# Transpositions of a two-layer FFN and attention kernel moved from TensorE to 16-bit DMA transposes

## The reference

```python
x = x + 0.5 * ffn(layernorm(x))          # 8 experts, hidden 256, all experts computed for all tokens
x = x + attention(layernorm(x))          # 8 heads of width 8, causal
x = x + 0.5 * ffn(layernorm(x))          # the same weights as the first
# ffn: logits = RMS-normalised xf @ gate_w.T + gate_b; g = top-1 of softmax(logits / 0.5)
#      norm_g = g / (g + 1e-6); h = gelu(xf @ w1 + b1); out = sum over experts of (h @ w2 + b2) * norm_g
# attention: layernorm again with weights, qkv = xn @ w_qkv; q, k scaled to unit length;
#      softmax(8 * q k^T, causal) @ v; @ w_out
```

## Time and profile before

| | us |
|---|---|
| median of 3 runs | 272.5 (272.35 to 272.63) |
| the profiled execution, its own time | 272.64 |
| its span in the profile | 271.2 |
| TensorE busy | 262.1 |
| VectorE busy | 220.5 |
| ScalarE busy | 218.8 |
| GpSimd busy | 81.1 |
| first FFN layer, by the windows | 8.7 to about 105 |
| attention | about 106 to 176 |
| second FFN layer | about 177 to 267 |

### The profile page before, as it was taken

One profiled execution on the slowest core, in us unless ns is written; L12 is line 12 of the kernel. 1 busy time (PEld: TensorE's weight loads), 2 busy tenths in 40 slices (PEclk: granted clock), 3 DMA queues, 4 the chain that ended last, 5 costly groups with the idle time before them and its releaser, 6 DMA issues.

```text
span 271.2 us, 5570 instructions
## 1 busy us (share of the span) xinstructions
PE 262.1 (97%) x1893; PEld 187.6 (69%) x1893; DVE 220.5 (81%) x599; ACT 218.8 (81%) x345; POOL 81.1 (30%) x178
## 2 busy tenths in 40 slices
PE   8999999999999999979998999999999999999995
PEld 7876878888788786533434534278888887888783
DVE  7999899998898979795687687478889678698784
ACT  2797678868877879999899999977777868859673
POOL 6202204214850483663148536430200000200100
PEclk9999999999999999999999999999999999999999
DMA  4641200001000100100010002300004211200311
GB/s 147 198 142 24 57 1 2 0 1 39 2 1 0 44 0 0 36 8 0 4 41 2 1 4 70 82 8 1 0 2 116 40 39 41 40 27 12 71 48 39
DMA packets 24895, 9.42 MB, mean 35 GB/s; under 512 B 15682, under 2 KB 24100, under 8 KB 24868
## 3 DMA queue, kind: packets, MB, share of 16 engines
q1 hardware_dynamic: 24724, 9.01, 13.4%
q10 hardware_dynamic: 144, 0.07, 0.1%
HBM read 4.88 MB, written 2.62 MB: 28 GB/s over the span
## 4 chain that ended last, share of the span: by engine, by line
PE 77%; ACT 6%; DVE 6%; issue 5%; POOL 4%; DMA 1%; POOLq 0%; DVEq 0%; ACTq 0%
PE ps L582 10%; PE ps L600 10%; PE ps L588 10%; PE ps L605 10%; PE ps L585 9%; PE ps L603 9%; PE ps L763 7%; ACT probs L968 3%; PE ps L725 3%; PE ps L797 2%; POOL probs L1593 2%; POOL w_raw L1587 2%; PE ps L702 1%; ACT h L955 1%; PE ps L543 1%
## 5 line engine op out<-in xcount | busy, mean ns | idle before, releaser
L955 ACT ACTIVATE h<-ps,cols 128x512 f32<-128x512 f32 x128 | 87.9, 694 | 35.8 <-PE ps L588 32.2
L1133 DVE TENSOR_TENSOR h_lo<-h,h_hi 128x512 fp32r<-128x512 f32 x128 | 88.1, 695 | 19.1 <-ACT h_hi L958 16.7
L968 ACT ACTIVATE probs<-ps 128x1024 f32<-128x1024 f32 (+1 forms) x80 | 65.4, 911 | 2.7 <-PE ps L725 2.5
L582 PE MATMUL ps<-xT_hi,w_hi 128*128 128x512 f32 x128 | 51.5, 402 | 0.0
L600 PE MATMUL ps<-h_hi,w_hi 128*128 128x512 f32 x128 | 50.6, 395 | 0.3 <-ACT yT L980 0.3
L605 PE MATMUL ps<-h_lo,w_hi 128*128 128x512 f32 x128 | 50.2, 392 | 0.0
L958 ACT ACTIVATE h_hi<-ps,cols 128x512 fp32r<-128x512 f32 x73 | 50.2, 688 | 0.0
L588 PE MATMUL ps<-xT_lo,w_hi 128*128 128x512 f32 x128 | 50.0, 390 | 0.0
L585 PE MATMUL ps<-xT_hi,w_lo 128*128 128x512 f32 x128 | 49.8, 389 | 0.0
L603 PE MATMUL ps<-h_hi,w_lo 128*128 128x512 f32 x128 | 49.8, 389 | 0.0
L763 PE MATMUL ps<-probs,v_ones 128*32 128x512 f32 (+4 forms) x384 | 34.2, 458 | 1.2 <-POOL probs L1593 1.0
(11 more groups left out here) (151 smaller groups left out, 288.5 us busy)
## 6 DMA issues: line engine op xcount, KB each, us to landing
w_raw<-in_L_ffn_w SPq DMA_DIRECT2D x8, 256.0 KB, 4.9
turned<-blocks SPq DMA_DIRECT2D x6, 256.0 KB, 2.1
w_raw<-turned SPq DMA_DIRECT2D x24, 64.0 KB, 2.3
w_raw<-v_ones SPq DMA_DIRECT2D x8, 128.0 KB, 2.4
x_sb<-in_L_attn_x SPq DMA_DIRECT2D x3, 256.0 KB, 7.3
out_x<-x_sb SPq DMA_DIRECT2D x3, 256.0 KB, 2.3
w_raw<-o_scaled SPq DMA_DIRECT2D x2, 256.0 KB, 4.5
x_sb<-in_L_attn_x SPq DMA_DIRECT2D x2, 128.0 KB, 2.2
```

The source lines that it names most:

```text
L582: pe.matmul(bank, w1_hi[:, w], xT_hi[:, cols_g], start=True, stop=False)
L955: first = nc.scalar.activation(h[:, slot, :], ps[:, BANK_H + slot, :], ACT.Gelu, bias=bias)
L968: nc.scalar.activation(probs[:, s % P_SLOTS, :, 0:width], ps[:, bank:bank + 2, 0:width], ACT.Exp, scale=SCALE).then_inc(exp_done, 1)
L1133: dve.tensor_tensor(h_lo[:, slot, :], h[:, slot, :], h_hi[:, slot, :].bitcast(f32), ALU.subtract).then_inc(split_done, 1)
```

## The change

1. The stacks of all four groups are turned by a DMA (`dma_start_transpose`, 16-bit, one for q and one for k, issued by SyncE after the group's `stack_done`). TensorE's transpositions, the four jobs, and the copies to `qT` and `kT` go; the layouts of `qT`, `kT`, `sq`, `qk_raw` and the small tensors change so that each operand is contiguous by group. `unit_vectors` becomes one instruction.
2. Three 128x512 tiles of fp32 are turned in another way: y of group 0, the attention norm of group 0, and the features (FFN norm) of group 3. GpSimd copies the tile as 16-bit halves in two planes (`make_planes`), SyncE turns the planes by one DMA, GpSimd joins them (`join_planes`) to `landed` or `xf`.
3. The order changes with it: the residual of group 0 to c = 6 and 7 of group 1, its attention statistics to 8 and 9, its norm to 12 and 13; the affine of its features, its qkv products and its copies into group 2; `high_stacks` of both groups into group 3; the jobs and the stacks of group 2 to earlier or later quads; GpSimd's program is written out.

```diff
-AT_ONE = dict(AT, gate_product=0)
-AT_THIRD = dict(AT, qk_transpose=13, q_copy=13, k_copy=13, ln_normalise=(2, 3), ln_transpose=5, ln_copy=5, ln_low=7,
-                att_normalise=(10, 11), qk_high=9, gate_product=5, gate_logits=6, gate_shift=12, gate_tanh=13, gate_weight=14)
+AT_ONE = dict(AT, gate_product=0, residual=(6, 7), att_stats=(8, 9), att_aggregate=10, att_normalise=(12, 13))
+AT_THIRD = dict(AT, ln_normalise=(2, 3), ln_transpose=5, ln_copy=5, ln_low=7,
+                att_normalise=(10, 11), gate_product=0, gate_logits=1, gate_shift=12,
+                first_affine=2, first_qkv=4, qk_squares=5, qk_copy=6, qk_sums=6, qk_guesses=7, gate_tanh=13, gate_weight=14)
...
-               qk_copy=1, qk_guesses=1, qk_high=8, qk_transpose=12, q_copy=12, first_scores=12)
+               qk_copy=1, qk_guesses=1, first_high=0, qk_high=9, first_scores=12)
...
-        jobs = [(q1, "ln", LAST), (q1 + 1, "project", (0, 0)), (q1 + 4, "project", (0, 1)),
-                (q1 + 5, "qkv", 0), (q1 + 6, "qkv", 1), (q1 + 7, "q_stack", LAST - 1), (q1 + 8, "k_stack", LAST - 1),
-                (q2, "q_stack", LAST), (q2 + 1, "k_stack", LAST), (q2 + 3, "ffn_ln", 0),
+        jobs = [(q1, "ln", LAST), (q1 + 2, "project", (0, 0)), (q1 + 4, "project", (0, 1)),
+                (q1 + 5, "qkv", 0), (q1 + 7, "qkv", 1), (q2 + 3, "ffn_ln", 0),
...
# SyncE
+            for n in range(3):
+                sp.wait_ge(planes_done, n + 1)
+                if n:
+                    sp.wait_ge(joined, n)
+                sp.dma_start_transpose(planes_t[:, :, :].rearrange("p w (t q) -> p (w t) q", q=P),
+                                       planes[:, :, :].rearrange("p w c -> p (w c)")).then_inc(planes_in[n], 16)
...
+                sp.wait_ge(stack_done, 2 * p + 2)
+                for turned_stack, stack in ((qT, q_stack), (kT, k_stack)):
+                    sp.dma_start_transpose(turned_stack[:, p, :, :].rearrange("p a (t q) -> p (a t) q", q=P),
+                                           stack[:, :, :].rearrange("p h r -> p (h r)")).then_inc(stacks_in[p], 16)
...
# ScalarE
+                if F == PLANED_FFN:
+                    act.wait_ge(xf_done[FFN], F + 1)
...
+                if p == PLANED_ATT:
+                    act.wait_ge(joined, 2)
+                    normed = landed[:, :]
...
# GpSimd
+            def make_planes(n, made, count, words):
+
+                pool.wait_ge(made, count)
+                if n:
+                    pool.wait_ge(planes_in[n - 1], 16)
+                pool.tensor_copy(planes[:, :, :], by_plane(words)).then_inc(planes_done, 1)
+
+            def join_planes(n, words):
+                pool.wait_ge(planes_in[n], 16)
+                return pool.tensor_copy(by_plane(words), planes_t[:, :, :])
...
+                if layer == 0 and g == 1:
+                    make_planes(0, y_evac, PLANED_Y + 1, yT[:, :])
+                    ln_once(2)
+                    join_planes(0, landed[:, :]).then_inc(joined, 1)
+                    gate_root(1)
+                    ln_twice(0)
+                    make_planes(1, xn_done[ATT], GROUP_TILES, xn[:, ATT, :, :].rearrange("p t d -> p (t d)"))
+                    ln_once(3)
+                if layer == 0 and g == 2:
+                    pool.wait_ge(resid, GROUP_TILES)
+                    join_planes(1, landed[:, :]).then_inc(joined, 1)
+                    make_planes(2, xn_done[FFN], GROUP_TILES * PLANED_FFN + GROUP_TILES,
+                                xn[:, FFN, :, :].rearrange("p t d -> p (t d)"))
+                    pool.wait_ge(gate_mm, PLANED_FFN)
+                    pool.wait_ge(xT_ready, PLANED_FFN)
+                    join_planes(2, xf[:, FFN, :]).then_inc(xf_done[FFN], 1)
+                    ln_twice(1)
+                    gate_root(2)
+                    inverse_lengths(pool, 0)
+                    unit_vectors(pool, 0)
+                if layer == 0 and last:
+                    low_parts(pool, 0)
+                    inverse_lengths(pool, 1)
+                    ln_twice(2)
+                    unit_vectors(pool, 1)
+                    low_parts(pool, 1)
+                    gate_root(3)
```

More of the change, by code:

```diff
@@ L190, in build @@
         blocks = sb("blocks", [P, GROUP])
+        u16 = mybir.dt.uint16
+        planes = sb("planes", [P, 2, GROUP], u16)
+        planes_t = sb("planes_t", [P, 2, GROUP], u16)
+        landed = sb("landed", [P, GROUP])
         turned_dram = [nc.dram_tensor(f"turned{n}", (P, GROUP), f32, kind="Internal").ap() for n in range(TURNS)]
@@ L232, in build @@
         o_zero = sem("o_zero")
+        planes_done, joined = sem("planes_done"), sem("joined")
+        planes_in = [sem(f"planes_in{n}") for n in range(3)]
         job_filled, job_emptied = sem("job_filled"), sem("job_emptied")
@@ L424, in low_features, with q_and_k, raw_tiles @@
             eng.tensor_tensor(xT_lo[:, part], features(F), xT_hi[:, part].bitcast(f32), ALU.subtract).then_inc(xT_ready, 1)
+        def q_and_k(qkv):
+            return qkv[:, :, 0:2 * INNER].rearrange("p t (w c) -> p t w c", c=ROW)
+        def raw_tiles(buffer, first):
+            return buffer[:, :, first:first + 2, :].rearrange("p w t c -> p t w c")
         def unit_vectors(eng, p):
@@ L635, in ffn_group @@
                         down(layer, F, 0)
-                        if operands and not first:
-                            y_transposes(F - 1, ln_groups=F + 1, att_groups=g - 1)
+                        if operands and g > 1:
+                            y_transposes(F - 1, ln_groups=LAST, att_groups=2 if last else 0)
                     if layer == 1 and first and c == 3:
@@ L913, in square_qk @@
                 for half, qkv in qkv_halves(p):
-                    nc.scalar.activation(sq[:, 2 * half:2 * half + 2, :], qkv[:, :, 0:2 * INNER], ACT.Square).then_inc(sq_done, 1)
+                    nc.scalar.activation(raw_tiles(sq, 2 * half), q_and_k(qkv), ACT.Square).then_inc(sq_done, 1)
             def copy_qkv(p):
@@ L918, in copy_qkv @@
                 for half, qkv in qkv_halves(p):
-                    nc.scalar.activation(qk_raw[:, 2 * half:2 * half + 2, :], qkv[:, :, 0:2 * INNER], ACT.Copy)
+                    nc.scalar.activation(raw_tiles(qk_raw, 2 * half), q_and_k(qkv), ACT.Copy)
                 if p == 0:
@@ L1073, in normalise @@
                 dve.wait_ge(rstd_done[kind], n + 1)
-                if n <= GROUPS:
-                    dve.wait_ge(ln_t[kind], n)
+                if kind == ATT and n:
+                    dve.wait_ge(planes_done, 2)
+                    dve.wait_ge(ln_t[ATT], n - 1)
+                elif kind == FFN and n == GROUPS:
+                    dve.wait_ge(planes_done, 3)
+                elif kind == FFN and n < GROUPS:
+                    dve.wait_ge(ln_t[FFN], n)
                 for i in tiles:
@@ L1166, in residual @@
                     xi = x_tile(g, i)
-                    y = y_rows(F) if landed else ps[:, bank, :]
+                    y = y_rows(F) if by_blocks else landed if F == PLANED_Y else ps[:, bank, :]
                     dve.scalar_tensor_tensor(xi, y[:, P * i:P * i + P], gate_half[:, F % 2, i:i + 1], xi,
@@ L1393, in empty @@
                     t0 = GROUP_TILES * LAST + halves[arg][0]
-                    dve.tensor_copy(qk_raw[:, halves[arg][0]:halves[arg][1] + 1, :], qkv[:, :, 0:2 * INNER])
+                    dve.tensor_copy(raw_tiles(qk_raw, halves[arg][0]), q_and_k(qkv))
                     for quad in range(QUADS):
@@ L1537, in ffn_group @@
                     ln_once(2 * GROUPS - 1)
-                if third:
-                    low_parts(pool, g - 2)
-                if layer == 0 and g == 1:
-                    ln_twice(g - 1)
-                    ln_once(F + 2)
             pool.memset(ones[:, :], 1.0).then_inc(const_self, 1)
```

222 lines of the change are left out of this document (83 added, 139 removed).

## The result

| | before | after |
|---|---|---|
| median (lowest to highest), us | 272.56 (272.35 to 272.63) | 275.96 (275.29 to 275.99) |
| ratio to before | | 1.012, 95% interval 1.0102 to 1.0138 |
| the profiled execution, its own time | 272.64 | 275.93 |
| its span | 271.2 | 274.2 |

The change made the kernel slower by 1.2%, 3.4 us, where the forecast was 0.8 us faster. The time lies near that of rival A (276.3 us), but not for the reason that A gave. The mean granted clock is 0.994.

What follows compares the result with a forecast made beforehand. TensorE (97% busy) was taken to bound the kernel, ScalarE's exponentials 108 to 134 us, both nearly thereafter. Layer -2.4, attention -1.2, stall +2.3, group 3 +0.4 sum to -0.9 us: 271.7 us, range 269.8 to 279 us.

Steps and rivals of the forecast that it cites:

- rival A: Transposing DMA takes 4.5 us, as the copy in short pieces; stall 5.9 us, total 276.3 us; chance 0.30.
- Stall 2.3 us: Group 2: TensorE waits 1.9 us for gelu 9 ahead of chunk 9's down-product, plus 0.4 us for backlog.
- the backlog: Group 2, after the stall: ScalarE still owes the qkv copies and VectorE its sums, 0.4 us more.
- C + T + C: Turns 2 and 3: GpSimd split, transposing DMA, GpSimd join, one after another; each GpSimd copy C taken as 1.2 us.
- T: Time of a 256 KB transposing DMA from issue to landing: taken as 2.5 us, between 2.1 and 11.3 us.
- VectorE's splits are early ... I count 0: Group 1: bunched residual, statistics and norm use some 1.5 us of split slack; counted 0, up to 1 us loss.
- Group 3: Attention's rstd stands ahead of the unit vectors on GpSimd, ScalarE's slot is a chunk later: 0.4 us lost.
- Attention: TensorE's 2.2 us of transpositions count only where ScalarE waits for scores, 134 to 151 us: 1.2 us gained.
- Groups 2 and 3 have over 5 us: Stacks' DMAs of groups 2 and 3 land with over 5 us to spare, so they are hidden.
- B: Rival: the DMA transposes blocks one by one, T near 11 us, stall 19 us, total near 300 us; chance 0.08.
- C: Rival: waits covered, GpSimd copy near 1.0 us, T 2.1 us, stall 0.3 us, total 268.9 us; chance 0.12.
- D: Rival: attention gives nothing, its waits come back elsewhere, the layer's gain is eaten: +0.3, 272.8 us; chance 0.15.

Runs made afterwards that it cites:

- experiment 10: Stacks-only kernel plus six SBUF to SBUF DMAs in SyncE's idle time (transposes of 1, 2, 4, 8 blocks; two plain 256 KB copies): 269.67 us.
- Experiment 3: Changed kernel plus eleven unused 128x128 fp32 products on TensorE between up 12 and down 9 of group 2: 275.19 us.
- Experiment 1: Changed kernel with ScalarE's rounding of group 3's features moved from chunk 5 to 9 of group 2, VectorE's low part from 7 to 11: 272.24 us.
- experiment 8: Stacks-only kernel plus five unneeded GpSimd copies of 128x1024 halves in group 1, where GpSimd's queue is idle: 274.03 us.
- experiment 5: Kernel of Experiment 1 with VectorE's low part of the features at chunk 9 instead of 11: 271.56 us.
- experiment 4: Changed kernel with only the stacks turned by DMA; y, norm and features turned by TensorE at the places of before: 269.69 us.
- experiment 6: Stacks-only kernel plus y of group 0 turned by planes, joined at once, with VectorE's residual at chunks 3 and 4: 270.5 us.
- experiment 9: Kernel of experiment 6 with planes split and joined by ScalarE instead of GpSimd: 270.8 us.

## Why the prediction was wrong

Right was the mechanism: where the stall comes, who makes it (two waits in ScalarE's queue, seen as 2.31 and 4.00 us), and the order in which norm, turn, affine, norm, turn and rounding follow each other. The term that failed is "Stall 2.3 us" (1.9 for the stop and 0.4 for the backlog): both together measured 6.3 us. What the traces have for it, in the prediction's own pieces:

| piece | predicted | measured |
|---|---|---|
| attention norm of group 0 done | 58.7 | 59.7 |
| first C + T + C | 4.9 | 6.0 (59.74 to 65.71) |
| affine, gelu 6 and rounding, split, norm 3 | 3.3 | 3.4 |
| second C + T + C | 4.9 | 5.6 (69.10 to 74.72) |
| rounding of the features, gelu 9 and its own, hand-overs | 2.5 | 1.9 |
| down 9 | 74.3 | 76.6 |

- **The stall, 1.9 forecast, 4.3 us measured.** From yT 0 to down 9 it is 39.61 us before and 42.43 us after, +2.8 us, though 1.47 us of TensorE's work are gone; the forecast for it was +0.4. T was 3.1 instead of 2.5 us (two of them, 1.2 us), and experiment 10 shows that this is the DMA's own time for 8 blocks. The norm was 1.0 us late: VectorE's half norm waited behind the gate weights and bunched work. The four copies took 5.1 us instead of 4.8. That is 2.5 us against the 2.4 that were missing.
- **The backlog, 0.4 forecast, 2.0 us measured.** From down 9 to yT 2 it is 10.54 us before and 11.67 us after, and the stacks' 0.91 us had left that stretch. I had counted what ScalarE owed of qkv, and not that VectorE too stands idle for 4.4 us behind ScalarE's wait and has norms, sums and low parts to work off beside each chunk's split. Experiment 3 shows that this backlog holds TensorE as long without the slow clock. Experiment 1 takes the stop at down 9 and its backlog away together, and group 2 gets 3.5 us shorter, not 6.3: ScalarE's first wait and VectorE's lateness stay.
- **"VectorE's splits are early ... I count 0"** was right for the time of group 1 in this kernel (23.01 us, 0.96 less than before, 0.88 forecast). What I had not considered is that GpSimd's copies slow VectorE itself. Where VectorE is busy without a gap this costs 0.6 us a copy (experiment 8). In the mended change (experiment 5) the four copies of group 2 lengthen VectorE's rows by 2.0 us in sum (a split at 59.87 us 1.40 us, a rounding at 69.18 us 1.07 us, a split at 73.90 us 1.13 us, a product at 65.09 us 0.42 us). How much of that reaches TensorE isn't shown: beside the first of these splits it has gaps of 0.3 us in sum, and from 68.1 to 81.5 us none.
- **Group 3**, 0.4 forecast, 0.54 us measured, by the mechanism named: ScalarE waits 0.57 us for the unit vectors, as before, but with its slot a chunk (1.36 us) later. Ahead of them GpSimd waits 0.93 us for VectorE's attention statistics, which wasn't in the forecast, and then makes the rstd.
- **Attention**, -1.2 forecast, -1.16 us measured, and the agreement is partly luck. The four waits of 1.6 us went, more than forecast; the first exponential comes 1.40 us after the start of the table load instead of 1.64, where the forecast had counted 0 for the stacks of group 1; and 0.3 us of a longer wait and the new one of 0.72 us go against it; the remaining 0.4 us lie in gaps too short to be listed. "Groups 2 and 3 have over 5 us" was wrong for group 3: it has none. The k stack landed late and cost ScalarE 0.72 us; where the same DMA landed 0.7 us earlier attention gave 1.7 us (experiments 3 and 4).
- **Sum**: -1.47 + 4.29 - 0.91 + 2.04 + 0.54 - 1.16 = +3.3 us, and -0.3 us from the second layer and the start, gives +3.0 us, the difference of the spans.
- **The rivals.** A priced the stall at 5.9 us with T at 4.5; the stall and its backlog were 6.3 us with T at 3.1. Its point of decision, 2.9 us, was passed by 0.2 us, which moves the forecast by 2 x 0.6 us to +0.3 us: most of the loss is from the other terms of the same sum. B is excluded by T, here and in experiment 10. C and D didn't come either: T was above C's 2.1 us, and attention gave 1.2 us. Of the signs of being wrong only the first came: T was over 2.9 us; no copy took more than 1.59 us, and VectorE held TensorE by 0.2 us in group 1. The two rules of the Trainium skill weighed there come out so: the blocks don't add up to the 10.5 us estimated from its 1309 ns ("VectorE: DVE Perf Modes", The three transpose paths), and the transposing DMA isn't as fast as the plain one either, as the Trainium skill has it ("Advanced Engine Details and Errata", X-Bar Transpose (TRN2)): 3.1 against 2.3 us.

## What to carry to other kernels

Where one in-order queue waits for two round trips over another engine and a DMA, add the whole chain up with all the hand-overs and look at what the wait leaves undone on each engine behind it; moving the wait's consumer four chunks later gave 3.7 us back for two numbers changed. A copy on an idle engine isn't free when a busy one is next to it: it cost 0.6 us where VectorE had no gap (experiment 8) and nothing that can be seen where it had slack (experiment 6), so look at what the busy one does meanwhile. Moving work to make room for a turn has a price of its own: 0.9 us on TensorE for a norm that came 1 us late (experiments 6 and 9). And take a change of several parts apart: here one part alone is 1% faster than the kernel before, and the other parts ate it.

## What the runs showed of the hardware

- While GpSimd copies 128x1024 16-bit halves (1.0 to 1.7 us each), VectorE's operations beside it take longer: most products of 128x32 0.85 to 1.07 us instead of 0.19 (that of 53.25 us in experiment 8 kept 0.18), two halves of a norm 2.16 instead of 0.60, a rounding of 128x512 0.8 to 1.2 instead of 0.42. The reduction at 54.43 us in experiment 8 kept its 0.19 us, and in after the residual at 64.42 us, with one operand in PSUM, kept its 0.60 us beside a join. That they share access to SBUF is stated by the Trainium skill ("GPSIMD Engine Reference", Specifications), with contention for VectorE instructions of two SBUF inputs or in a 2-port mode; the products agree with the first, and for the norm and the rounding no run here shows in which mode they are.
- The landing of the last transposing DMA of attention, issued at the same place, differed by some 0.7 us between executions (TensorE waited 0.90 and 0.20 us for it). What decides it stays open.
- A transposing DMA keeps SyncE's queue 1.2 to 1.3 us where a plain one of 256 KB takes 0.5 us, so that the second of a pair is issued 1.3 us after the first.
- After a stop of 2.2 us the granted clock went to 0.50 for some 3.4 us (up to 80.4 us, by the matmuls' distances); with a backlog on the engines that feed TensorE, preventing this gave nothing (experiment 3). After a wait of 2.2 us in experiment 8 the clock stayed at 1.00 in the profiled execution, and the seven executions with a mean of 0.992 to 0.994 took 1.4 us more. What decides whether it falls stays open.
